# Layer 0's s2 through DRAM, layer 3's weights summed in PSUM, and the last norm in two halves

## The reference

```python
# layer 0: graph attention
h = x @ W;  s1 = h @ a1;  s2 = h @ a2
e = leaky_relu(s1[:, :, None] + s2[:, None, :], 0.2) * adj
out = elu(softmax(e, axis=2) @ h + beta * h)
# layer 1: out = (adj @ x) @ weight + bias
# layer 2: masked attention with 8 heads, projection, then o + layernorm(o)
# layer 3: three gated steps
for _ in range(3):
    av = concat([adj @ h, adj @ h], -1)
    z  = sigmoid(av @ w3.T + h @ u3.T + biases)
    r  = sigmoid(av @ w4.T + h @ u3.T + biases)
    hv = tanh(av @ w5.T + (r * h) @ u5.T + biases)
    h  = (1 - z) * h + z * hv
```

## Time and profile before

| what | value |
|---|---|
| median of the runs | 1393.4 us |
| the profiled execution | 1397.72 us |
| its span, first to last instruction | 1395.9 us |
| PE busy | 1345.5 us (96%) |
| DVE busy | 1062.2 us (76%) |
| ACT busy | 790.0 us (57%) |
| POOL busy | 156.8 us (11%) |
| the chain that ended last | PE 88%, DVE 7%, the rest 5% |
| mean granted TensorE clock | 0.987 of full speed |

### The profile page before, as it was taken

One profiled execution on the slowest core, in us unless ns is written; L12 is line 12 of the kernel. 1 busy time (PEld: TensorE's weight loads), 2 busy tenths in 40 slices (PEclk: granted clock), 3 DMA queues, 4 the chain that ended last, 5 costly groups with the idle time before them and its releaser, 6 DMA issues.

```text
span 1395.9 us, 26919 instructions
## 1 busy us (share of the span) xinstructions
PE 1345.5 (96%) x10423; PEld 1143.7 (82%) x10423; DVE 1062.2 (76%) x2367; ACT 790.0 (57%) x1450; POOL 156.8 (11%) x196
## 2 busy tenths in 40 slices
PE   6789999999999999999999999999999999999996
PEld 5677888888888888888888888888888888887784
DVE  5778878877787777778788787878778776858455
ACT  2546656656565665556556555565656555654543
POOL 5101101010110111011010011101011110110000
PEclk8989999999999999999999999999999999999998
DMA  5001000000000000000000000000000100000000
GB/s 160 16 9 39 1 24 31 16 24 13 23 30 23 30 15 12 26 23 30 23 30 15 8 30 23 30 22 31 15 8 30 23 31 1 24 24 31 16 0 31
DMA packets 54653, 34.52 MB, mean 25 GB/s; under 512 B 34896, under 2 KB 51536, under 8 KB 54608
## 3 DMA queue, kind: packets, MB, share of 16 engines
q1 hardware_dynamic: 52800, 29.43, 7.0%
q0 software_dynamic: 1248, 3.94, 0.9%
q10 hardware_dynamic: 560, 0.52, 0.1%
HBM read 12.92 MB, written 8.39 MB: 15 GB/s over the span
## 4 chain that ended last, share of the span: by engine, by line
PE 88%; DVE 7%; ACT 2%; issue 1%; DMA 1%; POOL 1%; SPq 0%; POOLq 0%; ACTq 0%; DVEq 0%
PE banks L121 22%; PE banks L123 21%; PE banks L122 21%; PE banks L587 8%; PE banks L582 4%; PE banks L746 2%; PE banks L848 2%; PE banks L731 2%; PE banks L650 2%; PE banks L720 1%; PE banks L634 1%; DVE l_stats L245 1%; PE banks L642 1%; PE banks L709 1%; DMA ln_beta<-in_L_gnn_ln_beta_dram 1%
## 5 line engine op out<-in xcount | busy, mean ns | idle before, releaser
L1512 ACT ACTIVATE l_r<-banks,bias_r 128x512 f32<-128x512 f32 x90 | 61.8, 686 | 211.9 <-PE banks L123 211.6
L259 POOL TENSOR_TENSOR l_rstd<-l_mv,eps 128x4 f32<-128x4 f32 x48 | 20.5, 427 | 865.8 <-DVE l_mv L253 865.8
L1523 ACT ACTIVATE banks<-banks,bias_z 128x512 f32<-128x512 f32 x96 | 63.4, 662 | 55.0 <-PE banks L123 54.8
L1529 ACT ACTIVATE banks<-banks,bias_h 128x512 f32<-128x512 f32 x96 | 63.2, 659 | 46.6 <-PE banks L123 45.5
L2150 DVE TENSOR_TENSOR l_rh_lo<-l_r,l_rh_hi 128x512 fp32r<-128x512 f32 x90 | 60.0, 679 | 36.4 <-ACT l_rh_hi L1378 36.4
L273 ACT ACTIVATE y<-l_sum,l_offset,l_rstd 128x256 f32<-128x256 f32 x128 | 71.5, 592 | 11.1 <-DVE l_offset L267 11.1
L121 PE MATMUL banks<-l_rh_hi,u_hi 128*128 128x512 f32 x180 | 75.9, 422 | 0.9 <-DVE l_rh_lo L2150 0.7
L587 PE MATMUL banks<-adj_t,y 128*128 128x128 f32 x544 | 71.2, 279 | 1.7 <-ACT y L273 1.6
L123 PE MATMUL banks<-l_rh_lo,u_hi 128*128 128x512 f32 x180 | 71.0, 394 | 0.0
L122 PE MATMUL banks<-l_rh_hi,u_lo 128*128 128x512 f32 x180 | 70.8, 394 | 0.0
L587 PEld LDWEIGHTS banks<-adj_t,y 128*128 128x128 f32 x544 | 66.1, 194 | 5.7 <-issue 3.1
(11 more groups left out here) (296 smaller groups left out, 4357.5 us busy)
## 6 DMA issues: line engine op xcount, KB each, us to landing
x_tok<-in_x_dram SPq DMA_DIRECT2D x15, 512.0 KB, 3.5
l_res<-y SPq DMA_DIRECT2D x15, 512.0 KB, 2.9
out_dram<-l_res SPq DMA_DIRECT2D x15, 512.0 KB, 3.0
l_vpair<-l_vstage SPq DMA_DIRECT2D x32, 128.0 KB, 3.2
w_raw<-in_L_gnn_w_w_dram POOLq DMA_DIRECT2D x3, 512.0 KB, 8.0
qkv_raw<-in_L_gnn_w_qkv_dram POOLq DMA_DIRECT2D x1, 768.0 KB, 4.5
l_res<-in_x_dram SPq DMA_DIRECT2D x1, 512.0 KB, 5.0
u_raw<-in_L_gnn_u_w_dram POOLq DMA_DIRECT2D x2, 256.0 KB, 7.7
```

Source lines behind the costliest of these rows:

```text
L1512: nc.scalar.activation(own(u).r[:, m, :], rz(u)[:, m, :], ACT.Tanh, scale=0.5, bias=w.biases["r"][:, m:m + 1]).then_inc(s.r_ready.of(u), 1)
L1523: nc.scalar.activation(rz(u)[:, m, :], rz(u)[:, m, :], ACT.Tanh, scale=0.5, bias=w.biases["z"][:, m:m + 1]).then_inc(s.z_ready.of(u), 1)
L1529: nc.scalar.activation(hv(u)[:, m, :], hv(u)[:, m, :], ACT.Tanh, bias=w.biases["h"][:, m:m + 1]).then_inc(s.hv_ready.of(u), 1)
```

## The change

There are four parts in it. (1) From unit 4 on, `l0_diagonal` and `l0_spread` are gone. SP writes the s2 column of `l_h` to a small DRAM tensor when all four pieces are copied, waits for that, and reads it back twice, once for each graph's 64 partitions, so that each partition gets the 64 values of its graph for four tiles. DVE adds s1 to that tile. Units 0 to 3 still use the product. (2) `gate_sums` on GpSimd is gone: PE forms the transposed sums of the weights in PSUM, as products with the identity and, for "diff", with a negated identity that ACT makes at the start. The gates have a new order (diff first) and other PSUM banks, two of them are turned beside unit 0, and 28 of the 66 `keep_busy` transposes are gone. (3) The last unit's statistics, root, offset, norm and store are done in two halves; in each half ACT norms one tile and DVE the other. (4) The written-out orders of PE, ACT and DVE are new in fill, loop and drain, with small moves on SP and POOL.

```diff
+class SpreadSignal(Signal):
+    def at(self, u, n=None):
+        if by_tensor(u):
+            return self.sem, u + 1
+        return self.sem, u * self.per + (ON_TENSOR - self.per * (ON_TENSOR - 1))
+def by_tensor(u):
+    return isinstance(u, int) and u < ON_TENSOR
+ON_TENSOR = 4
+GATES = ("diff", "w4s", "w5s", "u3", "u5")
+BESIDE_UNIT_0 = 2
...
+        def l0_write_s2(u):
+            sp.wait_ge(*s.l0_h_ready.at(u, TILES))
+            sp.wait_ge(*s.l0_s2_done.at(u - 1))
+            sp.dma_start(s2_dram.rearrange("t p -> p t"), b.h[:, :, DIM + 1],
+                         allow_slow_non_contiguous=True).then_inc(s.l0_s2_ready.sem, 16)
+        def l0_read_s2(u):
+            sp.wait_ge(*s.l0_s2_ready.at(u))
+            sp.wait_ge(*s.l0_score.at(u - 1, 1))
+            for n in range(PER_TILE):
+                q = slice(n * NODES, (n + 1) * NODES)
+                rows = s2_dram[:, q].unsqueeze(0).to_broadcast([NODES, TILES, NODES])
+                sp.dma_start(b.s2_diag[q, :, :], rows).then_inc(s.l0_s2_done.sem, 16)
...
-        def gate_sums():
-            pool.wait_ge(w.loaded[3], 160)
-            for n in ("w3", "w4", "w5"):
-                nc.gpsimd.tensor_tensor(halves[n], halves[n], wide[n][:, :, DIM:2 * DIM],
-                                        ALU.add).then_inc(ws["summed"], 1)
-            pool.wait_ge(ws["summed"], 3)
-            nc.gpsimd.tensor_tensor(diff, halves["w3"], halves["w4"], ALU.subtract).then_inc(ws["natural"], 1)
...
         def turn_gate(i):
             if i == 0:
-                pe.wait_ge(ws["natural"], 1)
+                pe.wait_ge(w.loaded[3], 160)
+                pe.wait_ge(*s.l0_v.at(0, 2))
+            if i == BESIDE_UNIT_0:
                 pe.wait_ge(*s.l0_v.at(1, 2))
-            if i >= TILES:
-                pe.wait_ge(ws["gate_lo"], i - TILES + 1)
...
+                    for j, (rows, sign) in enumerate(terms):
+                        ins = nc.tensor.matmul(block, rows, sign[:, :], start=j == 0, stop=j == len(terms) - 1,
+                                               skip_group_check=True)
...
         def l1_product(u, t):
+            if is_first(u) and t % 2 == 0:
+                pe.wait_ge(ws["gate_lo"], 1 + t // 2)
...
# the order of PE in the loop, around layer 0
+            l3_candidate(i, 1, 0)
             f_turn(i + 1, 1)
-            l3_candidate(i, 1, 0)
+            l3_candidate(i, 1, 1)
             l0_turn(i + 3, 0)
             l0_turn(i + 3, 1)
-            l3_candidate(i, 1, 1)
...
         def l0_scores(u):
             dve.wait_ge(*s.l0_s2_done.at(u, 1))
-            nc.vector.tensor_tensor(b.e[:, :, :], front(u)[:, 0, 0:TILES * NODES].rearrange("p (t j) -> p t j", t=TILES),
+            on_psum = front(u)[:, 0, 0:TILES * NODES].rearrange("p (t j) -> p t j", t=TILES)
+            nc.vector.tensor_tensor(b.e[:, :, :], on_psum if by_tensor(u) else b.s2_diag[:, :, :],
...
+            for n in range(2):
+                l3_residual(15, n)
+                statistics_of_last(n)
+                last_norm.aggregate(dve, 15, n)
+            for n in range(2):
+                last_norm.take_offset(dve, 15, n)
+                apply_last(n)
```

More of the change, by code:

```diff
@@ L465, in l3_store, with store_last @@
             sp.dma_start(dst[u], own(u).res[:, :, :]).then_inc(s.stored.sem, 16)
+        def store_last(half):
+            two = pair_of(half)
+            sp.wait_ge(*s.y3.at(UNITS - 1, half + 1))
+            sp.wait_ge(s.y3_odd, half + 1)
+            sp.dma_start(dst[UNITS - 1][:, two, :], own(UNITS - 1).res[:, two, :]).then_inc(s.stored.sem, 16)
         def body(i):
@@ L1154, in drain @@
             l3_diff(12, 1, 1)
-            for n in range(4):
+            for n in range(3):
                 l0_project(15, n)
@@ L1343, in drain @@
             l3_diff(15, 2, 0)
+            for n in range(2):
+                l3_turn(14, 2, n)
             for n in range(2):
@@ L1551, in l3_apply, with apply_last @@
                 ins.then_inc(s.y3.sem, 1)
+        def apply_last(half):
+            last_norm.apply_on_scalar(act, UNITS - 1, half, own(UNITS - 1).res).then_inc(s.y3.sem, 1)
         def body(i):
@@ L1783, in fill @@
             l3_high(0, 1, 0)
-            for n in range(2, 4):
+            for n in range(1, 3):
                 l0_take_h(3, n)
@@ L1838, in drain @@
             l3_tanh(12, 0, 1)
+            l3_update_gate(12, 0, 1)
             l3_high(12, 0, 0)
-            l3_update_gate(12, 0, 1)
+            for n in range(2):
+                l3_take_h(12, 0, n)
             l3_high(12, 0, 1)
@@ L2072, in _ @@
+            l3_tanh(15, 2, 1)
+            l3_update_gate(15, 2, 1)
+            for n in range(4):
+                l3_apply(14, n)
+            for n in range(2):
+                apply_last(n)
         run(act, fill, body, drain)
@@ L2577, in fill @@
                 l0_share(0, n)
-            low_proj()
-            for n in range(2):
-                l0_low(1, n)
+            l0_low(1, 0)
+            low_qkv()
+            l0_low(1, 1)
             l0_add_h(0, 0)
@@ L2668, in fill @@
             l2_add_o(0)
-            for n in range(4):
+            for n in range(3):
                 l2_scale(0, n)
-            for n in range(4):
+            l2_residual(0, 0)
+            l2_scale(0, 3)
+            for n in range(1, 4):
                 l2_residual(0, n)
```

1465 lines of the change are left out of this document (750 added, 715 removed).

## The result

The changed kernel takes 1513.57 us (median of five, 1510.06 to 1516.95) against 1393.55 for the kernel before (five, 1392.13 to 1394.01): a ratio of 1.0862, 95% interval 1.0838 to 1.0886. It is 120 us slower. The profiled execution has a span of 1509.0 us, 113.1 more than that of the kernel before.

What follows compares the result with a forecast made beforehand. PE's instruction list bounds the loop, a chain of short dependent steps the fill. Gains of 8.5 (fill), 2.2 (loop), 1.3 (drain) and 2.0 (end) sum to 14.0: 1393.4 - 14.0 = 1379 us, own range 1374 to 1384, whole range 1370 to 1392.

Steps and rivals of the forecast that it cites:

- the write of s2: Loop, units 4 to 15: 512 runs of 4 bytes into DRAM, 32 per engine, were to take 1.9 to 2.0 us.
- The sign that the prediction had set for its own failure: Loop: the prediction fails if scores start over 6 us after the last copy of h; 4.5 to 4.9 was expected.
- The fourth rival: Loop: s2 late by the full bound, 3.2 us a transfer, PE waiting 2.8 per unit, 1409 us in all; chance 0.14.
- Reads: Loop: reading s2 back was to take 0.66 us for the second read's issue plus 1.4 + 0.3 for the read.
- Rest of the loop: Loop apart from the transfers; the whole loop was to gain net 0.2 us per turn, 2.2 us over eleven turns.
- the three new waits: Loop, PE: before f_turn 0.2 us, before the projection 0.2, for s2 before the attention's turn 0.3; 0.7 per turn.
- the forecast's 0.9 of savings: Loop, PE: removing the spread's issue, the wait behind it (0.68 us) and the wait ahead (0.22) saves 0.9 per turn.
- Fill: Start of the kernel, through the first units: 8.5 us gained, bounds 3 and 11.
- the order on ACT: Fill: unit 0's copies of h come ahead of weights' hi parts on ACT, gaining 4.5 us.
- three of the sums on GpSimd: Fill: without GpSimd's weight sums beside them, DVE's two attention products take 1.7 us less.
- Drain: Last units: PE waits 1.2 to 2.4 us for unit 15's y2 instead of 2.8 for unit 14; gain 1.3, bounds 0 and 2.8.
- End: Last norm and store in two halves: norm done 1.3 us earlier, half the last store's data; gain 2.0, bounds 1.0 and 2.3.

Runs made afterwards that it cites:

- e4: Kernel before with 36 single DMAs behind its last store, each three times and waited for alone; 512 neighbouring 4-byte runs into DRAM took 9.97 us.
- e2: Changed kernel with s2's 2 KB written as four runs of 512 bytes, so scores use other values (measures only): 1383.8 us, ratio 0.9923.
- e1: Changed kernel with the product on PE for every unit instead of s2 through DRAM: 1385.1 us, ratio 0.9938.
- e5: Kernel before with 36 more DMAs behind its last store, varying spacing and number of runs; 128 4-byte runs took 8.55 us at 4 bytes' distance.
- e3: Changed kernel, DVE first copying the four s2 values per partition into a tile, so the write has 128 runs of 16 bytes: 1398.8 us, ratio 1.0036.
- e6: Changed kernel writing s2's 512 values 64 bytes apart into an unread tensor, reads taking fixed contents (measures only): 1394.3 us, ratio 0.9998.
- e8: e3 with the turn of the attention half a gate later and the attention product behind another half: 1405.9 us, ratio 1.0084.
- e7: e1 with ACT's copies of unit 0's h back between the hi parts of weights at the start, as before the change: 1389.9 us, ratio 0.9967.
- e9: e1 with three of GpSimd's weight sums done again at the start, into a tile nobody reads: 1387.0 us, ratio 0.9961.

## Why the prediction was wrong

**The step that failed** is the write of s2, "32 per engine: 0.55 by packets, so 1.9 to 2.0". It took 9.0 in the median and up to 11.1. That is 7 us and more on a chain that by the forecast was already 0.3 us late, twelve times, with the low clock behind each wait: the wait of 0.3 became 9.0. The sign that the prediction had set for its own failure, scores over 6 us after the last copy, reads 255.78 - 242.58 = 13.2. The fourth rival named the right place: "512 writes of 4 bytes, neighbours in one DRAM row ..., then a read that waits for the last of them". That they are neighbours in DRAM is what the runs show; that they come from different engines was not tried. Its size was wrong: 3.2 per transfer, 1409 us. I took that end from the swap of v, but the swap writes runs of 128 bytes into SBUF, and e4 shows that even 4-byte runs into SBUF cost nothing of this kind (2.03 for 512). So it could not bound a write to DRAM. The store, which does write to DRAM, has long runs; its 1.4 beside the data was near for a write of that form (four runs: 1.17 to 1.27). For the write in question the trace had no row near, and my upper end was merely the slowest row I could find.

The Trainium skill ("DMA: Bandwidth & Descriptors", "Specifications") spoke against the change with its read-modify-write below 512 bytes, and I had given its rival 0.14. The runs agree in direction and add what decides: 128 runs of 4 bytes 64 or 512 bytes apart land in 1.44, the same as runs of 32 bytes side by side, so being short costs little by itself; being short next to another run costs 7 us. The fixed cost of about 2.0 us for one DMA, which the Trainium skill ("DMA: Bandwidth & Descriptors", "Anatomy of one DMA — SWDGE (gpsimd) path") gives for DMAs that GpSimd issues, is not what SP's write shows here: 1.17 to 1.27 for 2 KB in four runs.

**Reads**: forecast 0.66 + 1.7 = 2.4, measured 4.13 after the slow write and 3.55 in e2: 1.2 to 1.8 too small. One read alone takes 2.79 in e4, so 1.1 of that is the 1.7 itself. In e2 the fast write (1.27 in place of 1.9 to 2.0) and 0.2 of wakes make up for most of it: 4.9 from the last copy to the scores, against 4.5 to 4.9.

**Rest of the loop**: right in the sum, not in every term. PE had 9.7 us of cover (forecast 9.3), scores to attention took 4.8 (4.9). e2, where s2 is in time, has a turn 0.35 shorter than before, forecast 0.2. That the two numbers lie close is in part luck. Of the three new waits the one ahead of the projection is there with 0.2 (2.4 us in 12 in e1 and e2), the one for f_turn is not in the list of waits, and the one for s2 shows once, with 0.4. With 0.2 of new waits the forecast's 0.9 of savings would have given 0.7, so the savings were smaller than I took them as well as the waits.

**Fill**: forecast 8.5 earlier; layer 3 starts at 107.06 against 118.31, and at 107.35 and 110.04 in e1 and e2. The size fits, but I took it off the wrong sum. The execution profiled before was 4.3 us above the median, and its fill holds much of this: the same code starts layer 3 at 115.28 in e4 and at 112.19 in e5. Against the mean of the three, 115.3, the new fill (108.0 in the mean of six executions, those of the changed kernel, e1, e2, e3, e6 and e8; 105.8 to 110.0) gains 7.3; I subtracted from the median a gain worked out on a slow fill. The dummies that went cost nothing that shows: the clock of 0 to 128 us is 0.95 to 0.97 in those six executions, and 0.92, 0.95 and 0.97 in the three of the old fill. Of the parts, the order on ACT is worth 4.7 us (e7; forecast 4.5) and three of the sums on GpSimd 0.6 to 0.7 by the trace of e9, 1.9 by its median (forecast 1.7, on an operation that no longer stands beside them).

**Drain**: forecast 1.3 gained. PE's wait in e1 from 1090 us on:

```profile
PE banks L680 <- ACT y L290: 3.2, 1, 3.2
```

3.2 for y2 of unit 15 against 2.8 before, where 1.2 to 2.4 were expected: DVE has the reset and lo parts of unit 14 ahead of that norm. From the first product of layer 3 to the end e1 takes 1274.9 us and the kernel before 1277.6; with 11 x 0.14 from the loop and 2.3 from the end, first turn and drain together lost 1.1, where 1.3 gained was the forecast.

**End**: forecast 2.0, measured 13.1 - 10.8 = 2.3 in e1 and as much in e2. It is not the clock's: the last transposes took 1.68 before, 1.09 in e1 and 1.94 in e2. The norm is done 1.5 (e2) to 1.95 (e1) earlier against them, forecast 1.3; GpSimd's root takes 0.7 for two tiles, where it took 1.01 for four and I had left it equal.

So with s2 in time the whole change gains 10.3 (e2), where the forecast had 14.0; with the product in place of the transfers it gains 8.9 (e1). The rest of the error is one wait of 0.3 us per unit, which came out as 9.0 and, with the clock behind it, as 11.

## What to carry to other kernels

Before a value is sent through DRAM, look at how long its contiguous runs at the target are and how far apart: a scattered write of single 4-byte values side by side takes 8.6 to 11.1 us here from 128 values on, and with starts 16 bytes apart 128 runs land in 2.2 or less. Ask also where the row that you take for a bound writes to: here 4-byte runs into SBUF were cheap and into DRAM were not. A row of another shape is not a bound for such an operation; when a term stands on a dependent path with no slack, multiply its uncertainty by the number of turns before you give the forecast a range. And when the profiled execution is longer than the median, find out where before you subtract a gain from the median.

## What the runs showed of the hardware

- A write of 128 values of 4 bytes into neighbouring places in DRAM needs 8.6 to 9.0 us until it is reported as landed (e4, e5), one of 512 needs 10.0 alone and 8.9 to 11.1 in the loop, where the DMA engines show activity for the first 1.3 us only. 128 values 8 bytes apart 3.9, 16 apart 1.9, 64 apart 1.4. Into SBUF (2.0 for 512 values), or from DRAM into SBUF (2.2), none of it shows. Why 16 such runs take 2.0, 32 take 5.0 and 64 take 7.2 is open.
- After a wait of PE of 8.3 us the granted clock was 0.50 (1.2 GHz) for 3.5 us, after waits of 9.4 and 9.0 us for 6.0 us; where the attention was in time (e2) the loop from 128 to 1200 us had 1.00.
- Beside GpSimd's 128x512 sums, DVE's 128x512 operations that read SBUF alone took 1.05 and 1.12 us where they take 0.69 and 0.68 without them; those with an operand in PSUM kept their 0.68 and 0.74 (e9 against e1).
